# A macaron block of mixture-of-experts, linear attention and mixture-of-experts on one core: a group's rows placed one step earlier, 71 blocks of expert rows in place of 72, and no unread products in the attention stage

## The reference

```python
def ffn(h):                      # 8192 tokens
    top_v, top_i = top_k(h @ gate_w, 2)          # 2 of 8 experts
    p = softmax(top_v)
    expert_out = sum over the two: p * (silu(h @ Wg[e]) * (h @ Wu[e])) @ Wd[e]   # 128 -> 352 -> 128
    return expert_out + (silu(h @ Sg) * (h @ Su)) @ Sd                           # shared, 128 -> 176 -> 128

def attn(h):                     # 16 heads of 8, q and k through elu + 1
    kv, ksum = running sums over the 256 positions of k v^T and of k
    return (q kv / (q ksum + 1e-6)) @ W_proj + b_proj

x = x + 0.5 * ffn(layernorm(x))
x = x + attn(layernorm(x))
x = x + 0.5 * ffn(layernorm(x))
```

## Time and profile before

| | |
|---|---|
| time, median of 3 runs | 1247.82 us (1246.77 to 1250.56) |
| the profiled execution's own time | 1248.63 us |
| its span, from the first to the last instruction | 1246.6 us |
| granted TensorE clock, mean over the span | 0.923 |
| PE busy | 999.2 us (80%) |
| DVE busy | 900.7 us (72%) |
| POOL busy | 846.9 us (68%) |
| ACT busy | 673.8 us (54%) |

### The profile page before, as it was taken

One profiled execution on the slowest core, in us unless ns is written; L12 is line 12 of the kernel. 1 busy time (PEld: TensorE's weight loads), 2 busy tenths in 40 slices (PEclk: granted clock), 3 DMA queues, 4 the chain that ended last, 5 costly groups with the idle time before them and its releaser, 6 DMA issues. The chain is left out here.

```text
span 1246.6 us, 32188 instructions
## 1 busy us (share of the span) xinstructions
PE 999.2 (80%) x9076; PEld 750.5 (60%) x9077; DVE 900.7 (72%) x2377; ACT 673.8 (54%) x1474; POOL 846.9 (68%) x878
## 2 busy tenths in 40 slices
PE   2667655999999937788988898888864999999940
PEld 1444334899989924455555555555433899898940
DVE  6778783666766744788888888888854666666748
ACT  5556642555555623466666555666431555555545
POOL 4677773777777844467787787878642777777850
PEclk8889986999999967999999999999976999999975
DMA  9311121222222211001111111100003222222229
GB/s 280 104 49 49 54 85 55 79 77 76 82 75 76 74 56 34 17 29 42 34 34 35 49 36 38 42 19 17 20 33 82 77 78 77 78 74 77 73 89 332
DMA packets 69023, 86.89 MB, mean 70 GB/s; under 512 B 13164, under 2 KB 56625, under 8 KB 68974
## 3 DMA queue, kind: packets, MB, share of 16 engines
q1 hardware_dynamic: 51566, 52.41, 14.5%
q0 software_dynamic: 17408, 33.87, 8.2%
HBM read 45.01 MB, written 43.30 MB: 71 GB/s over the span
## 5 line engine op out<-in xcount | busy, mean ns | idle before, releaser
L489 POOL DMA_INDIRECT expert_results<-ey,eidx x288 | 299.6, 1040 | 70.8 <-issue 64.8
L481 POOL DMA_INDIRECT routed_rows<-row,idx x256 | 253.4, 990 | 73.6 <-issue 71.1
L1128 DVE SCALAR_TENSOR_TENSOR ehT<-eh,ehT 128x768 f16<-128x768 f32 x144 | 138.0, 958 | 151.6 <-ACT ehT L681 151.6
L676 ACT ACTIVATE esil<-PSUM 128x768 f32<-128x768 f32 x144 | 116.8, 811 | 236.3 <-PE PSUM L815 226.7
L813 PE MATMUL PSUM<-eT,WGU 128*128 128x256 f16 x864 | 237.7, 275 | 1.2
L814 PE MATMUL PSUM<-eT,WGU 128*128 128x256 f16 x864 | 237.4, 275 | 0.0
L815 PE MATMUL PSUM<-eT,WGU 128*128 128x256 f16 x864 | 237.4, 275 | 0.0
L503 POOL TENSOR_TENSOR space<-qk,val 128x1152 f32<-128x1152 f32 x64 | 138.3, 2172 | 73.7 <-DVE shift L1178 52.5
L813 PE MATMUL PSUM<-WD,ehT 128*128 x864 | 164.0, 221 | 7.8 <-DVE ehT L1128 5.2
L814 PE MATMUL PSUM<-WD,ehT 128*128 x864 | 162.6, 221 | 0.1
L815 PE MATMUL PSUM<-WD,ehT 128*128 x864 | 162.1, 220 | 0.0
(11 more groups left out here) (197 smaller groups left out, 2306.2 us busy)
## 6 DMA issues: line engine op xcount, KB each, us to landing
xe<-routed_rows SPq DMA_DIRECT2D x144, 130.0 KB
space<-expert_results SPq DMA_DIRECT2D x32, 512.0 KB, 4.1
expert_results<-ey,eidx POOLq DMA_INDIRECT x288
X<-in_L_attn_x_dram SPq DMA_DIRECT2D x16, 256.0 KB, 4.7
routed_rows<-row,idx POOLq DMA_INDIRECT x256, 2.3
out_dram<-X SPq DMA_DIRECT2D x16, 256.0 KB, 4.4
routed_rows<-pad_rows SPq DMA_DIRECT2D x24, 130.0 KB
space<-in_L_ffn_Wg_dram SPq DMA_DIRECT2D x1, 1408.0 KB, 9.1
```

The source lines that it names most:

```text
L481: pool.indirect_dma_start(routed, bass.IndirectOffsetOnAxis(ap=idx[u][:, k, j:j + 1], axis=0), row[u][:, j, :], None).then_inc(s_scattered ...
L489: pool.indirect_dma_start(result, bass.IndirectOffsetOnAxis(ap=eidx[u][:, h:h + 1], axis=0), ey[u][:, h, :], None, bounds_check=K * T - 1, ...
L676: act.activation(esil[u][:, :], PSUM[:, 1536 * u:1536 * u + 768], ACT.Silu, scale=2.0 ** -(SX + SWT)).then_inc(s_block_silu, 1)
L1128: return dve.scalar_tensor_tensor(out=dst, in0=src, scalar=float(2 ** scale), in1=high, op0=ALU.mult, op1=ALU.subtract)
```

## The change

Three edits. In the first stage DVE's `place(n + 1)` stands in step n, behind `choose(n + 1)` and `row_low(n + 2)`, and no longer at the start of step n + 1. In the attention stage the nine products of `keep_warm` are gone. In both block stages the last block, number 71 of 0 to 71, is not worked: the number of blocks that 8 experts can need is at most 71, since 16384 rows in blocks of 256 leave at most 7 more than 64. Where an engine did that block, it now counts its semaphores up once more behind a drain, so that all later counts stay as they are.

```diff
--- before.py
+++ after.py
@@ -371,6 +371,10 @@
 
             def load_block(f):
                 def step(n, v):
+                    if isinstance(n, int) and n == (f + 1) * NBLK - 1:
+                        sp.wait_ge(s_block_rows[v], (n - v) * (16 // XE))
+                        sp.drain().then_inc(s_block_rows[v], 16)
+                        return
 
                     m = n - f * NBLK
                     wait(sp, s_block_T, n - (XE - 1))
@@ -409,7 +413,7 @@
                 fours(sp, f * NBLK, (f + 1) * NBLK, load_block(f))
                 sp.drain().then_inc(s_phase, 1)
                 for u in range(2):
-                    sp.wait_ge(s_results[u], 16 * HALVES * NBLK // 2 * (f + 1))
+                    sp.wait_ge(s_results[u], 16 * HALVES * (NBLK // 2 - u) * (f + 1))
                 if f == 0:
                     pairs(sp, 0, NG, load_results)
 
@@ -483,6 +487,9 @@
 
             def results(n, u):
 
+                if isinstance(n, int) and n in (NBLK - 1, 2 * NBLK - 1):
+                    pool.drain().then_inc(s_carrier, 1)
+                    return
                 pool.wait_ge(s_block_results, n + 1)
                 pool.tensor_tensor(carrier[:, u:u + 1], ones32[:, 0:1], ones32[:, 0:1], ALU.mult).then_inc(s_carrier, 1)
                 for h in range(HALVES):
@@ -544,7 +551,7 @@
                 phase_end(pool, 2 * f + 1)
                 pairs(pool, f * NBLK, (f + 1) * NBLK, results)
                 for u in range(2):
-                    pool.wait_ge(s_results[u], 16 * HALVES * NBLK // 2 * (f + 1))
+                    pool.wait_ge(s_results[u], 16 * HALVES * (NBLK // 2 - u) * (f + 1))
                 phase_end(pool, 2 * f + 2)
 
         @block.scalar
@@ -692,7 +699,7 @@
 
             def res_value(n, u):
 
-                return (n - u) * (16 * HALVES // 2)
+                return (n - u) * (16 * HALVES // 2) - 16 * HALVES * u * ffn[0]
 
             def experts(f):
                 n0, n1 = f * NBLK, (f + 1) * NBLK
@@ -707,12 +714,16 @@
                 hi(n0, 0)
                 step(n0 + 2, 0)
                 step(n0 + 3, 1)
-                with act.Fori(0, (NBLK - 4) // 2) as i:
+                with act.Fori(0, (NBLK - 6) // 2) as i:
                     step(i * 2 + (n0 + 4), 0)
                     step(i * 2 + (n0 + 5), 1)
-                hi(n1 - 1, 1)
+                step(n1 - 2, 0)
+                hi(n1 - 2, 0)
+                results(n1 - 3, 1)
                 results(n1 - 2, 0)
-                results(n1 - 1, 1)
+                act.drain().then_inc(s_block_silu, 1)
+                act.drain().then_inc(s_block_high, 1)
+                act.drain().then_inc(s_block_results, 1)
 
             def attention_weights():
 
@@ -1030,10 +1041,13 @@
                     for b in range(PASS):
                         step(i * PASS + (2 + b), (2 + b) % XE, e)
                 e = [number(v) for v in range(XE)]
-                for m in range(2 + (NBLK - 4) // PASS * PASS, NBLK):
-                    step(m, m % XE, e, turn=m < NBLK - 1, read=m < NBLK - 1)
+                for m in range(2 + (NBLK - 4) // PASS * PASS, NBLK - 1):
+                    step(m, m % XE, e, turn=m < NBLK - 2, read=m < NBLK - 2)
+                block_down(n1 - 3, 1, e[1])
                 block_down(n1 - 2, 0, e[2])
-                block_down(n1 - 1, 1, e[3])
+                pe.drain().then_inc(s_block_turned, 1)
+                pe.drain().then_inc(s_block_products, 1)
+                pe.drain().then_inc(s_block_out, 1)
 
             def keep_warm(count):
 
@@ -1073,7 +1087,6 @@
                     gate_up(n - 1, 1 - u, 0)
                 if attend:
                     running_sums(m + 1, 0, 1)
-                    keep_warm(9)
                 if settle:
                     gate_up(n - 1, 1 - u, 1)
                 if attend:
@@ -1309,9 +1322,12 @@
                 with dve.Fori(0, (NBLK - 4) // XE) as i:
                     for b in range(XE):
                         step(i * XE + (n0 + 2 + b), (2 + b) % XE)
-                step(n1 - 2, 2)
-                step(n1 - 1, 3, ahead=False)
-                block_low(n1 - 1, 1)
+                step(n1 - 2, 2, ahead=False)
+                block_low(n1 - 2, 0)
+                dve.drain().then_inc(s_block_T, 1)
+                dve.drain().then_inc(s_block_hidden, 1)
+                dve.drain().then_inc(s_block_low, 1)
+                dve.drain().then_inc(s_block_places, 1)
 
             def combine_first(g):
 
@@ -1399,8 +1415,8 @@
             def first_ffn(n, v, i=None, b=None):
                 u = v % 2
                 edge = isinstance(n, int)
-                place(n, v, n)
                 if edge and n == 0:
+                    place(0, 0, 0)
                     deviations(3, 1, 4)
                 if edge and n == 1:
                     down_weights()
@@ -1416,9 +1432,12 @@
                 if not edge or n < NG - 1:
                     choose(n + 1, (v + 1) % 4, n + 1)
                 if edge and n == 0:
+                    place(1, 1, 1)
                     moments(1, 5)
                 if not edge or n < NG - 2:
                     row_low(n + 2, (v + 2) % 4)
+                if not edge or 0 < n < NG - 1:
+                    place(n + 1, (v + 1) % 4, n + 1)
                 if not edge or n > 0:
                     shared_add(n - 1, n - 1)
                 if edge and n == 1:
```

## The result

The changed kernel takes 1242.27 us (median of 12 runs, 1240.55 to 1244.86), the kernel before beside it on the same chip 1247.9 (median of 12 runs, 1246.41 to 1250.56): the ratio is 0.9957, with a 95% interval of 0.9948 to 0.9966. That is 5.6 us faster, where 11.3 were forecast. The time is in the range of 8 in 10 by a hair, and outside the forecast's own range of 1232 to 1241. The case that happened is the rival with a chance of 0.11: the clock falls in every second step.

What follows compares the result with a forecast made beforehand. POOL was taken to bound the first stage, no engine being full in the attention stage; 3.3 + 6.0 + 2.0 = 11.3 us gained gave 1236.5. Own range 1232 to 1241 (chance 0.60), range of 8 in 10 1229.5 to 1242.5.

Steps and rivals of the forecast that it cites:

- the rival with a chance of 0.11: Attention stage: the clock falls in every second step, so the stage gains nothing or loses up to 6 us: 1239 to 1245.
- The blocks: Both block stages: one block less in each gains 2.67 + 3.33 = 6.0 us, bounds 5.3 and 6.7; drains cost nothing.
- The place edit: First stage: earlier `place` shortens POOL's waits for `idx` and gains 3.3 us, bounds 0 and 8.8.
- waits under 4 us in all: First stage, sign in the profile after: POOL's ticket waits for `idx` sum to under 4 us in place of 8.8.
- From there on the pace is POOL's: First stage, after group 3: POOL sets the pace, having won 2.2 to 2.4 us by then, of 3.3 in all.
- The nine products with a whole clock: Attention stage: removing them gains 7.2 us in twelve steps of 26.8 each, 8.0 in all, if the clock never falls.
- `pk` would always end with POOL's outer product: Attention steps: coming 0.9 us earlier, DVE's `pk` always meets POOL's second L503 and ends 6.1 us into the step.
- over 1 us: Attention stage, sign in the profile after: `pk` takes over 1 us in most steps, ending 0.1 behind L503.
- The clock: Attention stage: longer PE idle stretches make the clock fall, four falls at 1.5 us each giving back 6.0 of the 8.0.
- I count one fall in the two first steps and three in the twelve regular ones: Attention stage: number of clock falls after the change, one in four steps, priced at 1.5 us each, 6.0 together.
- the growing wait for `xaT`: Regular attention steps: PE's wait of 1.19 us for ACT's `xaT` grows by about 0.9, endangering the clock.
- My rival with a fall in each step: Attention stage: without the nine products the clock falls in every step from the second; 13.2 us slower, 1261; chance 0.04.

Runs made afterwards that it cites:

- e2_blocks: The kernel before with 71 blocks per block stage as the only edit: 1242.41 us, ratio 0.9953 to the kernel before.
- e5_oneinput: The changed kernel with DVE writing the expert weights' low parts by a one-input copy instead of a two-input product: span 1240.5 against 1240.6 us.
- e7_fillproj: The changed kernel with the nine products back in the two first steps and four unread products ahead of PE's wait for `yaT`: 1229.46 us, ratio 0.9857.
- f1_nine: e7_fillproj with the nine products back in all steps, on another chip than its first run: 1242.54 us, ratio 0.9959 to the kernel before.
- f4_one: e7_fillproj with one unread product ahead of the wait for `yaT` in place of four: 1239.54 us, ratio 0.9938 to the kernel before.

## Why the prediction was right and where it was wrong

**The blocks: right.** 6.0 forecast; 6.6 in the two stretches of the changed kernel, 5.5 in the time of `e2_blocks`. The price of a block (3.33) is the same after, and the drains cost nothing that shows.

**The place edit: the moves right, the sum wrong.** Foreseen: the ticket of group 2 at 41.0 (it is at 41.07), that of group 3 at 55.4 to 55.7 (55.63), and that PE's `positions` don't hold `place` up. The waits for `idx` fell by 2.9, near the 3.3. (The sign that I named, waits under 4 us in all, contradicts that sum: 8.8 - 3.3 leaves 5.5, and 5.8 were measured.) The step that failed is "From there on the pace is POOL's": I took POOL's own work as fixed. It isn't. A ticket that meets DVE's weight conversion ends only 0.04 to 0.05 us behind it; before the change the conversions met DMA instructions alone, and now they meet two tickets as well. 2.2 of the 2.9 went back, 1.9 of it by these two tickets and most of the rest by the third. `e5_oneinput` shows the cause by taking the conversion's form away. The rows for it stood in the trace before, and I hadn't read them: of the DMA instructions beside the same conversion, the five that began 0.25 to 0.31 us behind its start took 1.41 to 1.47 us, the others 0.96. The prediction used one direction of a rule of the Trainium skill (SBUF — State Buffer, "Who interferes with whom"); this is the other: a DVE instruction with two inputs in SBUF blocks a GpSimd instruction that reads SBUF. The 77.26 row agrees in its end; its start does not, since the ticket begins 0.21 ahead of the conversion by the profile and was held up all the same. The page goes on to infer that such an instruction doesn't hold up the making of DMA descriptors. The DMA instruction of 1.63 us at 58.52, beside the conversion of 58.43 to 59.31, was held up here; since it also reads its row numbers (`idx`) from SBUF, the trace doesn't show which part of it stood still.

**The nine products with a whole clock: right in kind, too small.** Forecast 8.0 (7.2 in twelve steps, at 26.8 each). Measured against the kernel before: 328.83 - 319.26 = 9.6 in twelve steps, at 26.6 each. That `pk` would always end with POOL's outer product is confirmed for the whole clock: it ends 0.07 to 0.09 us behind it in all twelve steps of `e7_fillproj`. In the changed kernel it does so in seven; in the other five, which are the steps behind a fall, it ends behind POOL's addition. `pk` takes 0.7 to 0.95 us in `e7_fillproj`, less than the "over 1 us" of my sign. In the changed kernel `place` comes 4.8 to 5.1 us into the steps that don't stand behind a fall, where the forecast had it at some 4.5: PE's running sums (1, 0) now wait up to 0.25 us for DVE's `prod` in eight of the twelve steps, a wait that the forecast did not have. What is left in front of `place` is 0.43 in place of the 0.2 foretold. DVE's `pk` and the POOL instruction beside it, in `e7_fillproj`:

```profile
565.19 0.95 DVE L1227 TENSOR_TENSOR pk<-pick,posb 128x64 f32<-128x64 f32 x1
```

```profile
563.88 2.17 POOL L510 TENSOR_TENSOR space<-qk,val 128x1152 f32<-128x1152 f32 x1
```

They end at 566.14 and 566.05. In `f1_nine`, in a long step, `pk` begins at 593.25 and ends at 594.33, 0.08 behind POOL's addition (to 594.25), as in the earlier trace rows. All five steps of 27.9 there meet the addition, all of 26.5 to 27.1 the outer product, so most of the difference between them stands here.

**The clock: the price right, the number wrong.** The step that failed is "I count one fall in the two first steps and three in the twelve regular ones". There were two and six, and one more at 897.9; and the low clock that the kernel before has for 3.4 us from 910.8 lasts 6.8 us here, from 908.0. The price of 1.5 holds: 1.47 in `f4_one`, and (325.72 - 319.26) / 5 = 1.3 in the changed kernel against `e7_fillproj` (the sixth fall is paid behind the twelve steps). So of the 12.3 us that the attention stage wins with the clock whole (488.29 to 476.03 in `e7_fillproj`), 13.5 were given back (489.49 - 476.03: 3.1 ahead of the twelve steps, 6.5 in them, 3.9 behind them, where it isn't separated how much is the clock's), where the forecast had 8.0 and 6.0. I had taken the 3.3 us of idle time in the two first steps as the danger (PE waits 3.15 there now, and the clock did fall), and in the regular steps the growing wait for `xaT`. That wait did not grow: it stands at 1.19 as before. The wait that the fill of 0.9 us stood in is that for `yaT`, 1.30 us at the step's end, which the change doesn't touch and which I didn't name: with it filled the falls stop, and with 0.5 us in the one for `xaT` they don't. That this wait alone isn't enough is shown by the kernel before, where it stands unfilled and the clock falls in one step of twelve. The amount of unread products sorts the runs as well as their place does: 1.5 us in the middle of the step leave one fall and 0.9 ahead of `yaT` none, while 0.5 ahead of `xaT` leave seven and 0.2 ahead of `yaT` five. Which of the two it is, or the length of the steps (27.4 on the average before, 26.6 in `e7_fillproj`), is not settled by these runs.

The Trainium skill (TensorE: Matmul & The Clock Gate, "HAM oscillation") describes a kernel whose clock falls in every tile through one long wait for a DMA. The trace agrees with the back and forth and not with the length of the wait: in the regular steps here no wait of PE is longer than 1.4 us, and the clock falls. My rival with a fall in each step leaned on this page; the waits of this kernel are shorter than those of the page, and the falls came in half of the steps.

## What to carry to other kernels

Products that only keep the clock up belong where the engine waits anyway: four of them in a wait close ahead of the place where the clock fell brought 10 to 12 us, nine in the middle of the work cost about as much as they saved. How many are needed has to be tried: one in the same wait left five falls. When such products are taken out, look for the falls by step and not at the mean clock (0.923 and 0.920 here), and price a fall by the step behind it. When a wait of an engine is removed, ask what its instructions will meet at their new times: a one-column ticket took 1.13 us because of what DVE did beside it.

## What the runs showed of the hardware that was not expected

- In the changed kernel no wait of PE in the regular steps is longer than 1.4 us, and still PE ran for 3.4 us at 1.2 GHz in six of twelve, each time just behind waits of 1.3 and 0.5 us. 0.2 us of products in the first of these waits left five falls, 0.9 us none.
- A ticket of one column, 0.2 us elsewhere, took 1.13 us beside a product of 0.88 us on DVE whose two inputs lie in SBUF, and ended 0.04 us behind it. Ten DMA instructions of POOL (five before, five in the changed kernel) that began 0.1 to 0.4 us behind the start of such a product took 1.34 to 1.63 us in place of 0.96.
- The same kernel took 1386 us on one chip and 1247.6 to 1247.9 in all other comparisons.
